# Wide cross-attention in a decoder kernel: all eight PSUM banks and bf16 running maxima for the first unit of queries

## What is computed

```python
def _L1_xattn_ref(query, context, w_q, w_kv, w_out, b_out):
    NUM_HEADS = 16; HEAD_DIM = 64; SCALE = HEAD_DIM ** (-0.5)
    q = query @ w_q
    k, v = jnp.split(context @ w_kv, 2, axis=-1)
    ...
    scores = jnp.einsum('bhqd,bhkd->bhqk', q, k) * SCALE
    attn = jax.nn.softmax(scores, axis=-1)
    out = jnp.einsum('bhqk,bhkd->bhqd', attn, v)
    return out.transpose(0, 2, 1, 3).reshape(B, NQ, INNER) @ w_out + b_out

x = x + _L1_xattn_ref(_layernorm(x, axis=-1), ctx_768, L1_xattn_w_q, ...)
```

## Time and profile before

| | |
|---|---|
| device time, median of 3 runs | 4195.76 us (4195.39 to 4200.29) |
| the profiled execution, its own time | 4204.58 us |
| its span, first to last instruction | 4202.4 us |
| PE busy / DVE busy / ACT busy / POOL busy | 3694.7 / 2718.1 / 2076.1 / 2452.6 us |
| mean granted TensorE clock | 0.934 of 2.4 GHz |
| the block of the change | about 1840 to 3950 us of the span |
| of it, in front of the first exponential | 1840 to 1962.9 us |

### The profile page before, as it was taken

How to read it: one execution, slowest core, us unless ns; L and a number is a source line. 1 busy time by engine, 2 the same in 40 slices (tenths; PEclk the granted TensorE clock), 3 DMA queues, 4 the chain that set the end, 5 groups by cost and what they waited for, 6 DMA issues and landing times. The chain is left out here.

```text
span 4202.4 us, 57008 instructions
## 1 busy us (share of the span) xinstructions
PE 3694.7 (88%) x21368; PEld 1514.6 (36%) x21368; DVE 2718.1 (65%) x4201; ACT 2076.1 (49%) x2464; POOL 2452.6 (58%) x1245
## 2 busy tenths in 40 slices
PE   5875888888888888957999999999999999999699
PEld 2341222222222243423444444444444444444343
DVE  4547888888888323666677666766666766674232
ACT  2452888888888822511444444444444444444211
POOL 2205665656565200502888888878888888889700
PEclk6785999999999979856999999999999999999889
DMA  2013002001000010510011001110010001011100
GB/s 72 23 46 73 1 1 33 1 7 27 1 1 1 1 43 2 219 52 8 26 29 29 26 28 28 29 28 27 28 29 28 28 27 29 28 28 33 56 19 5
DMA packets 74152, 126.07 MB, mean 30 GB/s; under 512 B 10509, under 2 KB 26459, under 8 KB 73211
## 3 DMA queue, kind: packets, MB, share of 16 engines
q1 hardware_dynamic: 73308, 121.25, 10.1%
q10 hardware_dynamic: 576, 1.18, 0.1%
HBM read 87.76 MB, written 34.64 MB: 29 GB/s over the span
## 5 line engine op out<-in xcount | busy, mean ns | idle before, releaser
L1077 POOL TENSOR_TENSOR att_total<-att_total,att_prob 128x1024 f32<-128x1024 f32 x608 | 1569.7, 2582 | 332.6 <-ACT att_prob L1272 281.0
L1272 ACT ACTIVATE att_prob<-PS 128x1024 f32<-128x1024 f32 x816 | 791.6, 1022 | 1004.5 <-PE PS L1196 1000.7
L1289 DVE TENSOR_REDUCE att_top_piece<-PS 128x1 f32<-128x512 f32 (+1 forms) x1664 | 1036.7, 665 | 363.3 <-PE PS L1138 353.3
L647 DVE TENSOR_REDUCE att_top_piece<-PS 128x1 f32<-128x512 f32 (+4 forms) x1680 | 1020.5, 650 | 237.3 <-PE PS L450 141.7
L605 ACT ACTIVATE att_prob<-PS 128x1024 f32<-128x1024 f32 (+2 forms) x912 | 863.8, 1004 | 188.3 <-PE PS L489 151.8
L1209 PE MATMUL PS<-att_prob,att_vals 128*64 128x512 f32 x3264 | 791.9, 605 | 3.8 <-issue 2.9
L450 PE MATMUL PS<-cross_Kstack,cross_Qmax 49*128 49x512 bf16 (+1 forms) x1664 | 330.2, 391 | 187.8 <-DVE att_top_piece L647 165.8
L1138 PE MATMUL PS<-att_k_hi,att_q_hi 64*128 64x512 f32 (+1 forms) x1664 | 396.1, 468 | 87.2 <-DVE att_top_piece L1289 86.9
L515 PE MATMUL PS<-att_prob,cross_Vst 128*32 128x512 f32 x3264 | 443.7, 606 | 0.5 <-ACT att_prob L605 0.2
L382 POOL TENSOR_TENSOR att_stage<-att_stage,att_run 128x512 f32<-128x512 f32 x160 | 203.8, 1274 | 401.1 <-ACT att_stage L586 399.8
L450 PEld LDWEIGHTS PS<-cross_Kstack,cross_Qmax 49*128 49x128 bf16 x1664 | 92.8, 93 | 686.7 <-DVE att_top_piece L647 517.3
(11 more groups left out here) (246 smaller groups left out, 3252.3 us busy)
## 6 DMA issues: line engine op xcount, KB each, us to landing
att_vals<-values SPq DMA_DIRECT2D x192, 256.0 KB, 2.6
values<-mla_stage SPq DMA_DIRECT2D x24, 1024.0 KB, 4.2
f_w<-in_f_w SPq DMA_DIRECT2D x40, 256.0 KB, 4.8
cross_Kstack<-kparts SPq DMA_DIRECT2D x36, 204.0 KB
kparts<-att_prob SPq DMA_DIRECT2D x42, 128.0 KB, 1.8
att_vals<-values SPq DMA_DIRECT2D x16, 192.0 KB, 2.3
k_ctxT<-in_ctxT SPq DMA_DIRECT2D x1, 2448.0 KB
qparts<-att_prob SPq DMA_DIRECT2D x12, 128.0 KB, 1.8
```

The source lines that it names most:

```text
L647: dve.tensor_reduce(top_piece[:, n % 2, s * QT + qt, c:c + 1], PS[:, banks[item][s], 0:w], AX, ALU.max).then_inc(dve_freed, 1)
L1077: pool.tensor_tensor(so_far, so_far, prob[0:rows, j % RING, :, :], ALU.add).then_inc(summed, 1)
L1272: act.activation(prob[:, j % RING, :, :].rearrange("p a b -> p (a b)"), PSf[:, b:b + 2 * HALF], ACT.Exp, scale=scale).then_inc(exped, 1)
L1289: dve.tensor_reduce(top_piece[:, n % 2, s * QT + qt, c:c + 1], PS[:, bank(at + s), 0:w], AX, ALU.max).then_inc(dve_freed, 1)
```

## The change

In front of the steps, the banks are dealt out by hand. Maximum items go in turn to three slots of two banks (0 and 1, 2 and 3, 4 and 5; `SLOTS` = 3), q and k items to banks 6 and 7 in turn (`FILLS`), ("t", 0) to bank 4. Of a chunk's four query tiles, tile 0 is still reduced from PSUM by DVE. For tiles 1 to 3, ACT copies both banks in one instruction as bf16 (128x2x512), for chunk 0 straight into the tile's `run`, for the others into one of three `stage` buffers, and DVE merges `stage` into `run` with a maximum of two bf16 tiles; after the last chunk DVE reduces each `run` to two columns. `run` and `stage` lie in `prob`, which the steps use only later. DVE fills `top_piece` of unit 0 with -1e30 first. The six items of unit 1 no longer stand in `first`: unit 0's steps take them on, one more for every 8.5 steps, until the plan is level with the one before at the start of unit 1.

```diff
-    first += [("t", 0)] + maxima[PER_UNIT:PER_UNIT + AHEAD]
-    tiled, whole, taken, turned = [], [], PER_UNIT + AHEAD, 1
+    first += [("t", 0)]
+    tiled, whole, taken, turned = [], [], PER_UNIT, 1
...
-        goal = min(len(maxima), PER_UNIT * (n + 1) + AHEAD + -(-PER_UNIT * (kt + 1) // KT))
+        ahead = AHEAD if n >= 1 else AHEAD * (kt + 1) // KT
+        goal = min(len(maxima), PER_UNIT * (n + 1) + ahead + -(-PER_UNIT * (kt + 1) // KT))
...
+    FILLS, SLOTS = 2, 3
+    first_fills = [item for item in first if item[0] in ("q", "k")]
+    first_maxima = [item for item in first if item[0] == "m"]
+    first_bank, first_user = {("t", 0): PV}, {}
+    for i, item in enumerate(first_fills):
+        first_bank[item] = 6 + i % FILLS
+        first_user[item] = first_fills[i - FILLS] if i >= FILLS else None
+    for i, item in enumerate(first_maxima):
+        first_bank[item] = 2 * (i % SLOTS)
+        first_user[item] = first_maxima[i - SLOTS] if i >= SLOTS else None
...
+        run = [prob[:, i, 0, :].bitcast(BF16).rearrange("p (s n) -> p s n", s=2) for i in range(QT - 1)]
+        stage = [prob[:, i, 1, :].bitcast(BF16).rearrange("p (s n) -> p s n", s=2) for i in range(SLOTS)]
...
         def _(pe):
+            def wait_first(item):
+                if item in copy_number:
+                    pe.wait_ge(tile_copied, copy_number[item] + 1)
+                elif item is not None:
+                    pe.wait_ge(dve_freed, dve_count[item + (1,) if item[0] == "m" else item])
...
+            for item in first_maxima[-SLOTS:]:
+                wait_first(item)
             for j in range(0, STEPS, 2):
...
         def _(act):
             def side(item):
+                if item in copy_number:
+                    c, qt = item[2:]
+                    w = min(HALF, NCTX - c * HALF)
+                    act.wait_ge(side_filled, filled_count[item])
+                    if c == 0:
+                        to = run[qt - 1]
+                    else:
+                        i = merge_number[item]
+                        if i >= SLOTS:
+                            act.wait_ge(tile_merged, i - SLOTS + 1)
+                        to = stage[i % SLOTS]
+                    b = first_bank[item]
+                    act.activation(to[:, :, 0:w], PS[:, b:b + 2, 0:w], ACT.Copy).then_inc(tile_copied, 1)
...
         def _(dve):
             def side(item):
+                if item in copy_number:
+                    c, qt = item[2:]
+                    w = min(HALF, NCTX - c * HALF)
+                    if c == 0:
+                        return
+                    i = merge_number[item]
+                    dve.wait_ge(tile_copied, copy_number[item] + 1)
+                    if c >= 2:
+                        dve.wait_ge(tile_merged, i - (QT - 1) + 1)
+                    now = run[qt - 1][:, :, 0:w]
+                    dve.tensor_tensor(now, now, stage[i % SLOTS][:, :, 0:w], ALU.max).then_inc(tile_merged, 1)
+                    if c == MF - 1:
+                        dve.wait_ge(tile_merged, i + 1)
+                        dve.wait_ge(pieces_set, 1)
+                        dve.tensor_reduce(top_piece[:, 0, :, :].rearrange("p (s t) c -> p s t c", s=2)[:, :, qt, 0],
+                                          run[qt - 1], AX, ALU.max).then_inc(run_taken, 1)
+                    if (c, qt) == (MF - 1, QT - 1):
+                        dve.wait_ge(run_taken, QT - 1)
+                        dve.wait_ge(dve_freed, dve_count["m", 0, MF - 1, 0, 1])
+                        take_top(n)
...
+            dve.memset(top_piece[:, 0, :, :], MASKED).then_inc(pieces_set, 1)
```

More of the change, by code:

```diff
@@ L973, in attend_wide_heads @@
     hi_count = {}
-    for item in order:
+    FILLS, SLOTS = 2, 3
[8 more added lines that the diff above has]
+        first_user[item] = first_maxima[i - SLOTS] if i >= SLOTS else None
+    first_user["t", 0] = [item for item in first_maxima if first_bank[item] == PV][-1]
+    copy_number = {item: i for i, item in enumerate(item for item in first_maxima if item[3] > 0)}
+    merge_number = {item: i for i, item in enumerate(item for item in copy_number if item[2] > 0)}
+    ring_user = [first_user["t", 0], first_fills[-2 + len(first_fills) % 2], first_fills[-1 - len(first_fills) % 2]]
+    for item in first:
+        if item[0] == "m" and item not in copy_number:
+            dve_count[item + (0,)], dve_count[item + (1,)] = len(dve_count) + 1, len(dve_count) + 2
+        elif item[0] in ("q", "k"):
+            dve_count[item] = len(dve_count) + 1
+            hi_count[item] = len(hi_count) + 1
+        elif item[0] == "t":
+            negated_count[item] = len(negated_count) + 1
+    for item in order[len(first):]:
         place[item] = len(freed)
@@ L997, in attend_wide_heads, with bank_of @@
     dve_sums = [len([j for j in range((n + 1) * KT) if dve_adds(j)]) for n in range(UNITS)]
-    def bank(at):
-        return SIDE + at % BANKS
+    def bank_of(item, s=0):
+        return first_bank[item] + s if item in first_bank else SIDE + (place[item] + s) % BANKS
     def value_slot(n, f):
@@ L1124, in side @@
             def side(item):
-                at, kind, n = place[item], item[0], item[1]
-                wait_place(at)
+                kind, n = item[0], item[1]
+                alone = item in first_bank
+                if alone:
+                    wait_first(first_user[item])
+                else:
+                    wait_place(place[item])
                 if kind == "m":
-                    wait_place(at + 1)
+                    if not alone:
+                        wait_place(place[item] + 1)
                     c, qt = item[2:]
@@ L1143, in side @@
                     for qt in range(QT):
-                        ins = pe.transpose(PS[:, bank(at), qt * P:(qt + 1) * P], top[:, qt, :], ident[:, :])
+                        ins = pe.transpose(PS[:, bank_of(item), qt * P:(qt + 1) * P], top[:, qt, :], ident[:, :])
                 elif kind == "q":
@@ L1155, in side @@
                     c = chunk(f)
-                    ins = pe.matmul(PS[:, bank(at), 0:c.stop - c.start], wk[:, p % 2, :], ctxT[0:DC, c],
+                    ins = pe.matmul(PS[:, bank_of(item), 0:c.stop - c.start], wk[:, p % 2, :], ctxT[0:DC, c],
                                     start=True, stop=True)
@@ L1305, in side @@
                     dve.wait_ge(hi_copied, hi_count[item])
-                    dve.tensor_tensor(k_lo[:, n % 2, c], PS[:, bank(at), 0:c.stop - c.start],
+                    dve.tensor_tensor(k_lo[:, n % 2, c], PS[:, bank_of(item), 0:c.stop - c.start],
                                       k_hi[:, n % 2, c].bitcast(F32), ALU.subtract).then_inc(dve_freed, 1)
@@ L1312, in side @@
                     rows = flat(x[:, n % HALVES * QT:(n % HALVES + 1) * QT, :])
-                    dve.tensor_tensor(rows, rows, PS[:, bank(at), :], ALU.add).then_inc(dve_freed, 1)
+                    dve.tensor_tensor(rows, rows, PS[:, bank_of(item), :], ALU.add).then_inc(dve_freed, 1)
             def invert(n, i):
```

43 lines of the change are left out of this document (25 added, 18 removed).

## The result

| | before | after |
|---|---|---|
| median of the runs | 4200.3 us | 4176.1 us |
| ratio | | 0.9935, 95% interval 0.9918 to 0.9953 |
| span of the profiled execution | 4202.4 | 4167.0 |

A forecast was written before the change was run, and what follows sets the result against it. In front of the steps, PE-DVE handovers, four a chunk, were taken as the bound; PE in the steps. 38.8 us less in front and 8.8 more in the steps: 4195.8 - 30.0 = 4165.8 us, range 4149 to 4179.

The forecast's parts named there:

- What bounds the front: Front: four PE-DVE handovers a chunk; with the change one, closing a loop through the key chunk, 5.55 us instead of 8.24.
- Merges fit beside it at either end of their bound: Front loop: DVE's three merges a chunk, 0.7 us each or at most 1.22, fit within 5.55 us.
- The front's gain: In front of the steps: 2.4 us less at the start, 26.9 over ten chunks, 9.5 at the end; 38.8 together.
- the handover: Front loop: PE starts item D (tile 3) 0.19 us after DVE's reduces of tile 0.
- the three pairs of merge and reduce at the end: End of the front: three times a narrow merge, a DVE wait and a reduce of a `run`, 1.75 us each.
- The late items: Unit 0's steps: six added items, four at 1.36 us and two at 1.7, cost 8.8; from 2 to 13.
- the 1923.5 of the prediction: End of the front: sign that the first subtraction of maxima would stand near 1923.5 us in the trace.
- The forecast of the whole: Whole kernel: 38.8 us less in front, 8.8 more in the steps, net 30.0 us less.
- The clock rival: Front: PE's clock rises to 2.4 GHz, loop 4.3 us, whole 4150.3 if up throughout; chance 0.27.
- The loop was not longer: Front rival: late copies or waits make the loop 6.3 us a chunk; whole 4174 to 4178, chance 0.14.
- The late items did not come at PE's own time only: Unit 0's steps, rival: late items cost only PE's time, 7 us better than the sum, 4159; chance 0.08.
- The rival in which the banks don't help: Front: items still go hand over hand, loop near 8.24 us, whole 4195; chance 0.02.

The follow-up runs named there:

- key_early: The changed kernel with each key chunk moved one item earlier, ahead of item D (tile 3) of a chunk, in front of the steps; ratio to before 0.9874.
- merge_f32: The changed kernel with run and stage in float instead of bf16, so each merge takes 1.22 us; ratio to before 0.9923.
- after_again: The changed kernel, unaltered, run and profiled once more; ratio to before 0.9924.

## Why the prediction held, and where its terms were off

- **What bounds the front.** Right: one handover a chunk and a loop through the key chunk. 5.41 instead of 5.55 us; key_early is the proof, since moving only the key chunk's place breaks it and DVE becomes full instead.
- **Merges fit beside it at either end of their bound.** Right, by merge_f32.
- **The front's gain,** -38.8 forecast, -46.6 and -43.1 measured in the two profiles. Three things made it larger: the handover's 0.14 a chunk, 1.4 us; the three pairs of merge and reduce at the end, 1.59 instead of 1.75 each, 0.5 us (and the terms of that end add up to 17.6, not 17.7); and the clock, which was up for the first chunks in both profiles and for some later ones in the first. The forecast took half clock throughout and kept full clock as a rival; the truth was a mixture.
- **The late items,** +8.8 forecast, +12.7 measured. This is the term that was mis-sized. Its per-item prices held where the clock stayed up (1.35, 1.37, 1.6, and 0.9 around the 22nd); what it left out is that a wait of PE's can also cost the clock: 1.4 us around the 5th pair and 1.5 around the 26th, where it was also the third late item, for which the earlier trace rows had no case. Another 1.5 is the drop in the first two pairs, which not every execution has. As the upper bound I had 13, for another reason, a full item's time, and the forecast was to be called wrong if unit 0 gave back more than that: it stayed just inside. The first subtraction came at 1914.2, well before the 1923.5 of the prediction.
- **The forecast of the whole,** -30.0: by the runs -27 (-20 to -34) and, in the second set of runs, -32. That the sum came so near is in part luck: the front gave 4 to 8 us more than forecast and the steps took 4 more. The median itself, 4176.1, is 10 above the 4166 of the forecast; 4.5 of that is the kernel before, 4200.3 beside it instead of 4195.8.
- **The rivals.** The clock rival, priced as up throughout, came true in part. The loop was not longer. The late items did not come at PE's own time only. The rival in which the banks don't help fell at once. What I did not list as a case is that the eight banks alone would have given all of it, although the numbers for it stood in the prediction's rows: eight reduces at 0.60 to 0.66 and a low part are 5.4 to 5.9 us, about the loop.

## What to carry to other kernels

Where engines hand buffers around, write down the loop that one buffer's release closes, and ask of each instruction in it whether it is there by dependence or only by its place in the order: here a fill stood in it only because it came one item too late. Moving it alone gained nothing (79.6), the copies and the number format alone gained nothing (79.0 against 78.8), and together they took 18 us off the front (60.9). A relief for an engine that is not in the loop shows nothing until the loop is broken, so test such parts alone and together before judging them. Work moved out of an idle stretch into a full one has to be priced by the buffers it finds there, and by what the added waits do to TensorE's clock.

## What the runs showed of the hardware

- TensorE's clock fell from 2.4 to 1.2 GHz after PE had waited in the steps (busy 1.33 of 3 us from 1938, 1.62 of 3 from 2050.7, 1.68 of 3 from 1914), and the scores behind ran at half speed. The first two drops are in all eight profiles with that order of items. The third is in the five in which the clock had risen 0.4 to 0.7 us before the first subtraction, and in none of the eight, kernel before included, in which it rose 0.03 to 1.5 us after it. The changed kernel's front had the clock up in some later chunks in one profile and in none of them in the other, with the same instructions.
- In loops of steady length both levels were held: 0.50 through 49 us with PE busy 0.81 of the time in after_again's loop of 5.41, 1.00 in the 10 us shown with PE busy 0.72 in key_early's of 3.60. A busy PE at the lower level is partly busy because it is slow; why the one loop stayed low and the other high, these runs don't separate.
- ScalarE copied 128x1024 floats from two PSUM banks to bf16 in 1.02 us, as long as the exponential of the same tile to float.
- VectorE took a bf16 maximum of two 1024-wide tiles in 0.69 us, in float in 1.22, and a reduce of a 1024-wide bf16 tile in 1.22, no less than the float one in the earlier trace rows.
